# Search comparison as a sign on ScalarE, and the selection of four tiles in one comparison of 512 columns

## The reference

```
h = relu(layernorm(x))
agg = segment_sum(relu(h[src]), dst)
x1 = x + relu(relu((h + agg) @ W1 + b1) @ W2 + b2)
h = relu(layernorm(x1))
Q, K, V = relu(h @ Wq + bq), h @ Wk + bk, h @ Wv + bv          # 8 heads of 8
three hops over the edges of K and of the outer products K x V, each a
    norm-weighted segment_sum by dst; H = Q . M, scaled, times hopwise
out = x1 + V * hopwise[0] + the three H
```

## Time and profile before

| | |
|---|---|
| median of three runs | 1729.83 us |
| profiled execution, its time | 1737.73 us |
| profiled execution, its span | 1735.0 us |
| mean granted clock of TensorE | 0.89 of full |
| busy in the span: TensorE / VectorE / ScalarE / GpSimd | 75% / 86% / 59% / 69% |
| stage A in steady state | about 92 to 340 us, some 6.3 us a tick |
| stage B in steady state | about 385 to 615 us, 5.0 us a tick |

### The profile page before, as it was taken

The page is one execution under the profiler, slowest core; times in us unless marked ns, Lnnn a source line. Parts: engine busy times, 40 slices in busy tenths (PEclk is TensorE's granted clock), DMA queues, the critical chain, the costliest instruction groups (busy, mean ns, idle before and its releaser), DMA issues. The chain is left out here.

```text
span 1735.0 us, 22194 instructions
## 1 busy us (share of the span) xinstructions
PE 1301.4 (75%) x5794; PEld 800.3 (46%) x5794; DVE 1487.6 (86%) x3207; ACT 1017.0 (59%) x2815; POOL 1203.7 (69%) x1185
## 2 busy tenths in 40 slices
PE   3788888878888858777771777776588999777771
PEld 2666666656555534554550333323233444454551
DVE  5999999979999958999997999996456788799991
ACT  4688887858999954554552455553455666333330
POOL 7777766707777517777744777774777777777776
PEclk9799999979999967988895899899799999988886
DMA  5255554425666547999995788886345545466640
GB/s 130 80 115 114 127 123 113 127 70 147 159 170 157 145 93 249 317 320 314 305 313 183 271 308 305 300 307 242 92 124 155 158 135 154 132 177 173 176 138 16
DMA packets 281219, 313.83 MB, mean 181 GB/s; under 512 B 169009, under 2 KB 198569, under 8 KB 268550
## 3 DMA queue, kind: packets, MB, share of 16 engines
q1 hardware_dynamic: 224166, 246.39, 45.8%
q0 software_dynamic: 56928, 66.04, 15.0%
HBM read 214.54 MB, written 161.32 MB: 217 GB/s over the span
## 5 line engine op out<-in xcount | busy, mean ns | idle before, releaser
L946 PE MATMUL bank<-product,ident 128*128 128x512 f32 (+1 forms) x800 | 382.5, 635 | 137.6 <-DVE product L1302 137.5
L549 POOL DMA_INDIRECT state<-state_hop,slot_of_src x392 | 395.2, 1008 | 126.1 <-issue 108.0
L719 ACT ACTIVATE bank<-state,norm 128x512 f32<-128x512 f32 x392 | 251.2, 679 | 254.2 <-DMA state<-state_hop,slot_of_src 218.0
L1302 DVE TENSOR_TENSOR product<-bank,queries 128x512 f32<-128x512 f32 x392 | 261.9, 689 | 91.3 <-ACT bank L719 89.6
L946 PEld LDWEIGHTS bank<-product,ident 128*128 128x128 f32 x800 | 160.6, 206 | 357.7 <-issue 183.7
L511 POOL DMA_INDIRECT x_edges<-in_x,dst_tiles x196 | 203.5, 1039 | 106.2 <-issue 53.9
L525 POOL DMA_INDIRECT row_of_src<-node_rows,pos_int x196 | 195.3, 996 | 104.1 <-issue 54.3
L511 POOL DMA_INDIRECT x_edges<-in_x,src_tiles x196 | 210.0, 1071 | 75.1 <-issue 55.2
L565 POOL DMA_INDIRECT out<-rows,dst_out x196 | 193.3, 986 | 59.7 <-issue 58.8
L1300 DVE SCALAR_TENSOR_TENSOR acc<-acc,same_as_before,bank 128x512 f32<-128x512 f32 x196 | 145.7, 744 | 15.1 <-ACT bank L719 14.7
L1113 DVE SCALAR_TENSOR_TENSOR acc<-acc,same_as_before,bank 128x512 f32<-128x512 f32 x196 | 145.8, 744 | 1.7
(11 more groups left out here) (220 smaller groups left out, 2992.1 us busy)
## 6 DMA issues: line engine op xcount, KB each, us to landing
state_hop<-acc SPq DMA_DIRECT2D x98, 1024.0 KB, 4.6
x_nodes<-in_x SPq DMA_DIRECT2D x49, 256.0 KB, 4.2
src_row<-in_src_row SPq DMA_DIRECT2D x49, 256.0 KB, 3.9
out<-out_rows SPq DMA_DIRECT2D x49, 256.0 KB
dst_row<-in_dst_row SPq DMA_DIRECT2D x49, 256.0 KB, 3.4
kv_rows<-kv SPq DMA_DIRECT2D x49, 256.0 KB, 3.1
gg<-head_sums SPq DMA_DIRECT2D x98, 128.0 KB
kv_back<-kv_rows SPq DMA_DIRECT2D x49, 256.0 KB
```

The costliest lines, as they stand in the source:

```text
L549: pool.indirect_dma_start(out=mg[u % 4][:, k, :], out_offset=None, in_=d_m[hop - 1], in_offset=bass.IndirectOffsetOnAxis(ap=sidx[:, t:t + ...
L719: act.activation(pw[t % len(pw)][:, :], mg[u % 4][:, k, :], ACT.Copy, scale=wn12[:, t:t + 1]).then_inc(weighted, 1)
L946: ins = ten.matmul(ph[:, 0:k * D].rearrange("p (c j) -> p c j", j=HD), ident[:, :], part, start=(r == 0), stop=(r == HD - 1))
L1302: vec.tensor_tensor(ihj(pr[m % 2][:, u % 2 * EH + k, :]), ihj(pw[t % len(pw)][:, :]), over_j(Q[:, t, :]), ALU.mult).then_inc(multiplied, 1)
```

## The change

It touches three things.

- The comparison of the search (L1204) leaves VectorE. ScalarE makes it as `Sign(src - first dst + 0.5)`, so +1 or -1 in place of 1 or 0, after its square of the gathered rows (L678), within the same tick. To make the matmul give the same row, `delta` is halved and gets an offset: its first row is half the sum of the first and the last partition's destinations, and the last column is T/2 (for partition 0, T/2 + (P-1)T/2).
- For that the prologue loads one more row of 784 bytes (`N_LOADS` 15), and VectorE gets a negation, a halving, a column `rowb` and a second small memset.
- The four comparisons L1134 become one `tensor_tensor` over 128x512, with each tile's own destinations broadcast along the columns, after the variance step L1198.

```diff
-        N_LOADS = 14
+        N_LOADS = 15
@@ sync: prologue loads
             for to, what in ((dpm[:, :], dst_pm), (dprev[1:P, :], dst_pm[0:P - 1, :]),
+                             (dprev[0:1, :], dst_pm[P - 1:P, :]),
@@ scalar: after the square of x_edges (L678)
+                u = g - 1
+                if 0 <= u < CU:
+                    if u == 0:
+                        act.wait_ge(consts_set, 1)
+                    act.wait_ge(srow_in[u % 3], landed(u, u % 3, 3))
+                    wait(act, searched, u - 1)
+                    act.activation(gsel[u % 2][:, :], srow[u % 3][:, :], ACT.Sign, bias=rowb[:, 0:1]).then_inc(g_set, 1)
@@ vector: prologue
-            own.add(vec.memset(dprev[0:1, :], 0.0))
-            own.add(vec.memset(delta[:, T:T + 1], float(T)))
+            step(vec.memset(delta[:, T:T + 1], T / 2))
+            own.add(vec.memset(delta[0:1, T:T + 1], T + (P - 1) * T / 2))
             own.sync()
             vec.wait_ge(cleared, 1)
             vec.wait_ge(loaded, 16 * N_LOADS)
+            step(vec.tensor_scalar(dprev[0:1, :], dprev[0:1, :], -1.0, None, ALU.mult))
             step(vec.tensor_tensor(delta[:, 0:T], dpm[:, :], dprev[:, :], ALU.subtract))
+            own.add(vec.tensor_scalar(delta[:, 0:T], delta[:, 0:T], 0.5, None, ALU.mult))
+            own.add(vec.tensor_scalar(rowb[:, :], dpm[:, 0:1], -1.0, 0.5, ALU.mult, ALU.add))
@@ vector: each tick
-                def select(n):
-                    ...
-                            ins = vec.tensor_scalar(sel[u % 2][:, k * P:(k + 1) * P], drow[u % 3][:, k * P:(k + 1) * P],
-                                                    tmf[:, t:t + 1], None, ALU.is_equal)
-                    ...
                     own.add(vec.reciprocal(qp[:, 4, lo:hi], qp[:, 3, lo:hi]))
-                    select(1)
                     own.sync()
@@
                     own.add(vec.tensor_tensor(q[:, 2, lo:hi], q[:, 0, lo:hi], q[:, 0, lo:hi], ALU.mult))
-                    select(1)
                     own.sync()
                     own.add(vec.scalar_tensor_tensor(q[:, 2, lo:hi], q[:, 1, lo:hi], float(D), q[:, 2, lo:hi],
                                                      ALU.mult, ALU.subtract))
-                    select(1)
                     own.sync()
                     vec.tensor_scalar(q[:, 2, lo:hi], q[:, 2, lo:hi], 0.0, None, ALU.max).then_inc(varred, 1)
-                    select(1)
-                u = g - 1
-                if 0 <= u < CU:
-                    vec.wait_ge(srow_in[u % 3], landed(u, u % 3, 3))
-                    wait(vec, searched, u - 1)
-                    vec.tensor_scalar(gsel[u % 2][:, :], srow[u % 3][:, :], dpm[:, 0:1], None, ALU.is_ge).then_inc(g_set, 1)
+                u = g - S0
+                if 0 <= u < AU:
+                    vec.wait_ge(drow_in[u % 3], landed(u, u % 3, 3))
+                    wait(vec, turned_e, u - 1)
+                    vec.tensor_tensor(sel[u % 2][:, :].rearrange("p (k c) -> p k c", c=P),
+                                      drow[u % 3][:, :].rearrange("p (k c) -> p k c", c=P),
+                                      tmf[:, u * EH:(u + 1) * EH].unsqueeze(2).to_broadcast([P, EH, P]),
+                                      ALU.is_equal).then_inc(s_set, 1)
```

More of the change, by code:

```diff
@@ L198, in gnn @@
         st = [sb(f"stats{b}", [P, 6, COLS]) for b in range(RS)]
+        rowb = sb("row_begins", [P, 1])
         epsc, warm = sb("eps_col", [P, 1]), sb("root_of_one", [P, 1])
@@ L1121, in _ @@
                 qp, q = st[(g - 1) % RS], st[g % RS]
-                n_sel = 0
-                def select(n):
[L1126 to L1133, removed]
-                            ins = vec.tensor_scalar(sel[u % 2][:, k * P:(k + 1) * P], drow[u % 3][:, k * P:(k + 1) * P],
-                                                    tmf[:, t:t + 1], None, ALU.is_equal)
-                        n_sel += n
-                        if n_sel == EH:
-                            ins.then_inc(s_set, 1)
                 if g - 1 in STAT_NO:
@@ L1147, in _ @@
                                              ALU.mult, ALU.mult).then_inc(scaled, 1)
-                else:
-                    select(1)
                 m = DENSE_AT.get(g - 8)
```

## The result

The changed kernel takes 1761.68 us (median of four runs, 1756.69 to 1765.75), the kernel before 1734.05 us beside it: 27.6 us more, a ratio of 1.0155, 95% interval 1.0104 to 1.0206. The forecast, 1746, had the direction and most of the mechanisms, but the measured time lies above its range (1727 to 1760). The loss, forecast at +16.3, is +27.6.

The account below looks back on a forecast made before the run. It took stage A's VectorE to wait on ScalarE's root behind the comparison, with stores lacking margin. Terms -0.7 + 1.0 + 6.5 + 1.0 + 2.4 + 6.1 = +16.3 us gave 1746 us, range 1727 to 1760.

Parts of the forecast that it names:

- What bounds the kernel: VectorE looked like stage A's bound, but its comparison only covered an equally long wait for ScalarE's root; stores had no margin.
- Part 1: Stage A, comparison leaves VectorE: nothing gained in usual ticks, as the reciprocal still waits for the root; -0.7 us in all.
- The term -0.7 for the long comparisons: Stage A: about five of 40 steady ticks, with comparisons of 0.68 us, gain 0.13 us each.
- Part 2: Sign on ScalarE in stage A: free in steady ticks, 0.5 us each in three already late ticks; +1.0 us.
- a rival (0.26): Stalls at stores drag the clock down, some 0.6 us more in 13 cycles: +24 us, 1754 us; chance 0.26.
- Part 3: SyncE's queue in stage A: load released about 1.3 or 0.78 us later, stores behind it late, VectorE stalls; +6.5 us.
- Part 4: Start: prologue +1.0 us for an extra load and short steps; first ticks net +2.4 us (bounds 0 and 4).
- the preparation ticks: First ticks 6, 7 and 9: long preparations follow the comparison on VectorE, so its time is truly saved, 1.4 us.
- Part 5: Stage B selection: one long comparison delays the reciprocal, 0.40 us more per three-tick cycle; +6.1 us (bounds 0 and 10).

Follow-up runs that it names:

- the comparison over 64 columns: Kernel before with the search's comparison still on VectorE but over 64 of its 512 columns; tenth to fiftieth variance step 252.7 us against 255.4.
- the kernel with both mends: Changed kernel with stores ahead of the source-row load in SyncE's order and five small matmuls ahead of TensorE's wait for the Sign; ratio to before 1.0047.
- the early Sign: Changed kernel with the Sign moved ahead of the square root in ScalarE's tick, selection still one comparison; ratio to before 1.0015.
- the fastest version: Changed kernel with Sign ahead of the root, four selection comparisons back, VectorE's PSUM additions ahead of the reciprocal, SyncE's stores first; ratio to before 0.9875.

## Why the prediction was right and where it failed

- **What bounds the kernel; Part 1.** The mechanism was right: the reciprocal stayed 0.55 us after the variance step, and the comparison over 64 columns shows that it had covered the wait. The term -0.7 for the long comparisons had the wrong sign: in 11 of the 40 ticks it is now the variance step that takes about 0.39 in place of 0.18 (at 210.33), which costs 2.3 us. The 0.2 us that sat in the comparison moved to the instruction ahead of it. By the Trainium skill, "SBUF — State Buffer", section "Who interferes with whom", both are of the kind that can contend with GpSimd. The trace agrees and shows with what: in each of the 11 ticks GpSimd's indirect load of edge rows (L513) had begun 0.57 to 0.64 us before the variance step and was still running, and the five long comparisons of the kernel before had one (L511) begun 0.55 to 0.59 us before them. Where such a load had begun 0.46 or 0.83 us before, the step took 0.18, so it depends on how the two fall; why just so is not shown.
- **Part 2, the step that failed.** It priced the Sign in steady ticks at nothing beside late ticks, and TensorE's later start as covered "by about 0.5 us at full clock". That held at full clock only. TensorE's idle time before the Sign is followed by half clock; then L853 and the matmuls behind it end late, ScalarE waits 11.9 us for turned blocks, and roots are late. The sum had +1.0 here and nothing for the clock; measured are 4.0 to 5.7 us for half clock in stage A, and 2.0 that the kernel with both mends still pays for half clock just ahead of it. At full clock about 0.9 is left for the Sign, near the forecast's +1.0. I had the mechanism as a rival (0.26), but tied it to the stalls at the stores; the gap before the Sign was enough, since 27 us at half clock stay when no store is late, where the kernel before in the same order has none. (TensorE stands idle ahead of its work for up to 1.5 us at a time in the former and for 0.9 in nearly every tick of the latter.) The Sign was also 0.1 us longer than its nearest row.
- **Part 3.** The mechanism was right in each link: SyncE released 1.39 us later in such a tick (1.98 less 0.59; forecast 1.3), the store behind it late, VectorE waiting for it in 11 places. Forecast +6.5, measured +5.2 beyond the kernel before (3.5 if the clock is mended first). What I did not see is that the kernel before already paid 9.5, where the rows showed 6.0 of waits.
- **Part 4.** The prologue was 0.6 in place of 1.0 (-0.1 to +1.8 over the runs with the same prologue). The first ticks were mis-sized: +5.3 in place of +2.4. Up to the sixth variance step the loss was 5.5 against my 3.8, and of the 1.4 us that were to come back in the preparation ticks only about 0.3 did. With the early Sign the first ticks lose 2.0, so 3.3 of it is the late place.
- **Part 5.** The mechanism was right, the size somewhat low: +8.3 in place of +6.1, +7.5 as time when alone, with an interval (+4.9 to +10.3) that takes in the forecast. The mean of the six stages B with the new selection is 7.1 us above the mean of the four with the old one in the gaps and the additions in their old place. A regular cycle grew by 0.51, not 0.40. ScalarE now waits 0.3 us for the later L1201 in one tick of three; that this is the difference is not shown.

The sum missed by 11.3 us (+27.6 against +16.3). By stages, which come to +28.0, the miss is 7.7 in stage A, 2.9 in the first ticks and 2.2 in stage B, less 1.1 in the prologue and between the stages. In stage A, where most of it lies, half clock has 6.0 by the split above.

## What to carry to other kernels

An instruction that ends together with the answer it precedes is cover, not cost; taking it away changes nothing until other work is put in its place. When an operation moves to another engine, follow its semaphore to every queue that it releases: here a load, and behind it the stores. And in an engine with idle time look for where in its tick the idle time is: the same Sign took 23 us more of stage A behind the root than before it, and before it cost 1 us against the kernel before with stores first.

## What the runs showed that was not expected

- Five useless matmuls in each tick made stage A of the changed kernel 5.7 us shorter (4.0 with the stores first); TensorE's clock then stood at 0.99 in place of 0.92 (at 1.00 in place of 0.95).
- A store's visible waits understate its price: 10.2 us of waits, 14.7 us of stage A; in the kernel before 6.0 and 9.5. With the extra matmuls, where hardly any half clock follows a stall, the two are close: 12.0 and 13.0.
- An instruction of VectorE that takes 0.2 us longer beside GpSimd's indirect load can pass this on to its neighbour when it is taken away, and onto a more costly place: 5 long comparisons at 0.13 became 11 long variance steps at 0.2.
- A Sign over 512 columns with a column as bias took 0.704 to 0.766 us in the changed kernel, a square over as many columns 0.61.
- The gains of an order hold for a pace: the fastest version has 0.9875 beside a kernel before of 1741 us and 1.0031 beside one of 2076 us, while the late Sign with early stores and extra matmuls has 1.0047 and 0.989.
